# Embedding tower on one core: sixteen tables picked by one-hot matmuls instead of fourteen, the gathers in equal banks, and the dots of three blocks moved in front of the last turns

## The reference

```
e = stack of tbl_f[ids[:, f]] over f          # (512, 32, 128)
dot = einsum('bnd,bmd->bnm', e, e)            # all pairs of features
z = dot[:, iu, ju]                            # the 496 pairs above the diagonal
h = concatenate([z, dense_ctx], axis=1)       # (512, 512)
h = maximum(h @ W_top1 + b_top1, 0)           # 512 -> 512
h = maximum(h @ W_top2 + b_top2, 0)           # 512 -> 256
y = h @ W_top3                                # 256 -> 1
```

## Time and profile before

| | us |
|---|---|
| time of the kernel before, median of 3 runs | 121.43 |
| lowest and highest of them | 121.08, 122.03 |
| span of the profiled execution | 149.4 |
| in it, busy: TensorE matmuls | 118.9 |
| VectorE | 76.3 |
| ScalarE | 79.4 |
| GpSimd | 72.0 |

### The profile page before, as it was taken

The page is one execution under the profiler, slowest core; times in us unless marked ns, Lnnn a source line. Parts: engine busy times, 40 slices in busy tenths (PEclk is TensorE's granted clock), DMA queues, the critical chain, the costliest instruction groups (busy, mean ns, idle before and its releaser), DMA issues.

```text
span 149.4 us, 2614 instructions
## 1 busy us (share of the span) xinstructions
PE 118.9 (80%) x1008; PEld 95.5 (64%) x1008; DVE 76.3 (51%) x106; ACT 79.4 (53%) x128; POOL 72.0 (48%) x80
## 2 busy tenths in 40 slices
PE   0689993599996998798799931289829899999994
PEld 0568871268773875486566721289729788998972
DVE  2999961199969996984969000013103033123411
ACT  3699674199939969999999300030512112210022
POOL 3787777278747747747747777300550720000000
PEclk9999999569999999999999996559986999999999
DMA  4798763136763587379511121102471731015000
GB/s 136 248 335 306 234 207 97 35 61 212 225 205 81 190 263 239 72 241 311 170 35 47 50 55 50 47 0 72 136 222 35 202 77 41 7 35 171 9 0 1
DMA packets 10990, 19.29 MB, mean 129 GB/s; under 512 B 2385, under 2 KB 7377, under 8 KB 10978
## 3 DMA queue, kind: packets, MB, share of 16 engines
q1 hardware_dynamic: 7234, 12.96, 27.9%
q0 software_dynamic: 2304, 4.72, 11.7%
q10 hardware_dynamic: 1440, 1.44, 2.8%
HBM read 17.02 MB, written 2.13 MB: 128 GB/s over the span
## 4 chain that ended last, share of the span: by engine, by line
PE 66%; issue 15%; DVE 11%; ACT 4%; DMA 2%; DVEq 1%; SPq 0%
PE two_ps L562 16%; PE two_ps L564 14%; DVE onehot L327 8%; PE free_ps L604 8%; PE two_ps L623 8%; PE two_ps L604 7%; PE turn_ps L572 4%; DVE low L310 3%; PE free_ps L634 3%; PE two_ps L634 2%; ACT emb L403 2%; DMA home<-picked 2%; PE two_ps L639 1%; PE turn_ps L623 1%; DVEq L364 1%
## 5 line engine op out<-in xcount | busy, mean ns | idle before, releaser
L301 POOL DMA_INDIRECT rows<-tables,row_no x64 | 63.4, 991 | 39.4 <-issue 18.0
L562 PE MATMUL two_ps<-onehot,high 128*128 128x512 f32 x118 | 50.9, 432 | 12.6 <-DVE low L310 5.2
L564 PE MATMUL two_ps<-onehot,low 128*128 128x512 f32 x118 | 48.2, 408 | 1.3 <-issue 1.3
L327 DVE TENSOR_TENSOR onehot<-pick_id,free_ps 128x1536 fp32r<-128x1536 int16 (+2 forms) x25 | 41.5, 1662 | 6.4 <-remote 5.2
L562 PEld LDWEIGHTS two_ps<-onehot,high 128*128 128x128 f32 x118 | 23.4, 198 | 23.7 <-issue 15.1
L564 PEld LDWEIGHTS two_ps<-onehot,low 128*128 128x128 f32 x118 | 23.6, 200 | 5.5 <-issue 1.5
L310 DVE TENSOR_TENSOR low<-home,high 128x512 fp32r<-128x512 f32 (+1 forms) x33 | 20.8, 631 | 8.6 <-issue 6.3
L420 ACT ACTIVATE away<-pick_id,less_row 128x512 f16<-128x512 int16 x34 | 22.3, 712 | 0.0
L604 PE MATMUL free_ps<-emb 128*64 128x64 f32 x272 | 12.7, 231 | 11.8 <-issue 10.5
L435 ACT ACTIVATE onehot<-away 128x512 fp32r<-128x512 f16 x34 | 19.2, 622 | 2.0 <-remote 1.9
L604 PEld LDWEIGHTS free_ps<-emb 128*64 128x64 f32 x272 | 10.7, 140 | 14.0 <-issue 11.9
(11 more groups left out here) (38 smaller groups left out, 63.2 us busy)
## 6 DMA issues: line engine op xcount, KB each, us to landing
home<-picked SPq DMA_DIRECT2D x10, 512.0 KB
home<-picked SPq DMA_DIRECT2D x3, 640.0 KB
pick_id<-pick_ids SPq DMA_DIRECT2D x12, 128.0 KB
w_sb<-w SPq DMA_DIRECT2D x3, 512.0 KB
dot_out<-home SPq DMA_DIRECT2D x10, 128.0 KB, 2.3
rows<-tables,row_no POOLq DMA_INDIRECT x64
dot_out<-home ACTq DMA_DIRECT2D x6, 128.0 KB, 2.5
pairs<-dot_out SPq DMA_DIRECT2D x10, 64.0 KB, 2.0
```

The source lines that it names most:

```text
L301: pool.indirect_dma_start(rows[:, k % ROWS_HELD, i, :], None, lone[i] if one_table else tables, bass.IndirectOffsetOnAxis(ap=id_sb[:, 0, c ...
L327: dve.tensor_tensor(onehot[:, c % HOT:c % HOT + n, :], ids, own, ALU.is_equal).then_inc(onehot_dve, n)
L562: pe.matmul(out, high[:, at, D * k:D * (k + 1)], onehot[:, c % HOT, :], start=(k == 0), stop=False)
L564: pe.matmul(out, low[:, at, D * k:D * (k + 1)], onehot[:, c % HOT, :], start=False, stop=(k == KR[t] - 1)).then_inc(picked_done, 1)
```

## The change

PICK goes from 14 to 16: two more tables of 1250 rows (20 chunks) are picked, and 16 tables are gathered. The leftover banks with their two tensors `lone0` and `lone1` are gone: a block is 4 banks of 4 tiles, 16 banks and 64 gathers in all, and every gather takes its row number from `row_no`. BY_ACT has new numbers for tables 11 to 15: 3, 3, 3, 4, 4 instead of 4, 4, 4. Bank t - 3 (LAG) is turned and copied behind pick t instead of bank t - 1. So banks 0 to 12 are turned among the picks. Dot groups 0 to 5 and `dot(6, 0)` follow right behind with no turns between them, then layer 1 of blocks 0 and 1, and only then turns 13 and 14 and the halves of bank 15, in the places that 17, 18 and 19 had. The same is done on ScalarE. `dot` waits for one bank more with each half group.

```diff
--- before.py
+++ after.py
@@ -8,7 +8,7 @@
         1250, 12500, 1250, 1250, 1250, 12500, 12500, 1000, 1000, 1000, 1250, 1250, 1000, 1000,
         1000, 1250, 1250, 1250]
 
-PICK = 14
+PICK = 16
 PICKED = sorted(range(F), key=lambda f: (ROWS[f], f))[:PICK]
 GATHERED = [f for f in range(F) if f not in PICKED]
 SLOTS = GATHERED + PICKED
@@ -33,7 +33,7 @@
 LOWS = [cut(KR[0], [PIECE])] + [cut(k, LOW_CUT) for k in KR[1:]]
 LOW0 = [sum(len(p) for p in LOWS[:t]) for t in range(PICK + 1)]
 
-BY_ACT = [2, 1, 2, 2, 2, 2, 2, 2, 3, 2, 2, 4, 4, 4]
+BY_ACT = [2, 1, 2, 2, 2, 2, 2, 2, 3, 2, 2, 3, 3, 3, 4, 4]
 
 ALONE, AHEAD = 2, 2
 
@@ -48,13 +48,11 @@
 
 
 TB, SUB = 4, 32
-MORE = GF - 4 * TB
-BANKS = 1 + BLK // SUB
+BANKS = BLK // SUB
 NB = BLOCKS * BANKS
-TILES = [TB if k % BANKS else MORE for k in range(NB)]
-TILE0 = [sum(TILES[:k]) for k in range(NB + 1)]
-
-TURNED = PICK - 1
+TILES = NB * TB
+
+LAG = 3
 TABLES_HELD, IDS_HELD, HOT, AWAY, ROWS_HELD = 3, 4, 16, 8, 4
 
 CTX = 16
@@ -68,7 +66,7 @@
 PARTS = [(0, 2), (2, 3), (3, 4)]
 
 
-def build(nc, row_ids, pick_ids, tables, lone0, lone1, picked, context, w1, w2, small, y):
+def build(nc, row_ids, pick_ids, tables, picked, context, w1, w2, small, y):
     f32, f32r, i32, i16 = mybir.dt.float32, mybir.dt.float32r, mybir.dt.int32, mybir.dt.int16
     ALU = mybir.AluOpType
     ACT = mybir.ActivationFunctionType
@@ -83,10 +81,9 @@
         def sem(name):
             return ctx.enter_context(nc.semaphore(name))
 
-        lone = [lone0, lone1]
         ident = sb("ident", [P, P], f32)
-        id_sb = sb("id_sb", [P, 2, TILE0[NB]], i32)
-        row_no = sb("row_no", [P, TILE0[NB]], i32)
+        id_sb = sb("id_sb", [P, 2, TILES], i32)
+        row_no = sb("row_no", [P, TILES], i32)
         rows = sb("rows", [P, ROWS_HELD, TB, D], f32)
         emb = sb("emb", [P, B, F], f32)
 
@@ -289,18 +286,15 @@
             pool.wait_ge(ident_ready, 1)
             pool.affine_select(out=ident[:, :], in_=ident[:, :], compare_op=ALU.not_equal, fill=1.0,
                                base=0, pattern=[[-1, P]], channel_multiplier=1).then_inc(ident_ready, 1)
-            pool.wait_ge(row_ids_in, 16)
+            pool.wait_ge(row_no_ready, 1)
             for k in range(NB):
-                if k == 1:
-                    pool.wait_ge(row_no_ready, 1)
                 if k >= ROWS_HELD:
                     pool.wait_ge(turned, k - ROWS_HELD + 1)
-                for i in range(TILES[k]):
-                    c = TILE0[k] + i
-                    one_table = k % BANKS == 0
+                for i in range(TB):
+                    c = TB * k + i
                     pool.indirect_dma_start(
-                        rows[:, k % ROWS_HELD, i, :], None, lone[i] if one_table else tables,
-                        bass.IndirectOffsetOnAxis(ap=id_sb[:, 0, c:c + 1] if one_table else row_no[:, c:c + 1], axis=0)
+                        rows[:, k % ROWS_HELD, i, :], None, tables,
+                        bass.IndirectOffsetOnAxis(ap=row_no[:, c:c + 1], axis=0)
                     ).then_inc(late_rows_in if k == NB - 1 and i >= TB // 2 else rows_in[k % ROWS_HELD], 16)
 
         @block.vector
@@ -447,14 +441,8 @@
 
             def emb_out(k):
                 act.wait_ge(turned, k + 1)
-                r, u = divmod(k, BANKS)
-                if u == 0:
-                    out = emb[:, BLK * r:BLK * (r + 1), 4 * TB:GF]
-                    in_ = turn_ps[k % 2][:, 0:MORE * P].rearrange("p (f b) -> p b f", f=MORE)
-                else:
-                    b0 = BLK * r + SUB * (u - 1)
-                    out = emb[:, b0:b0 + SUB, 0:4 * TB].rearrange("p b (i f) -> p i b f", i=TB)
-                    in_ = turn_ps[k % 2][:, :].rearrange("p (i b f) -> p i b f", i=TB, f=4)
+                out = emb[:, SUB * k:SUB * (k + 1), 0:GF].rearrange("p b (i f) -> p i b f", i=TB)
+                in_ = turn_ps[k % 2][:, :].rearrange("p (i b f) -> p i b f", i=TB, f=4)
                 copy(out, in_).then_inc(emb_ready, 1)
 
             def dots_out(grp):
@@ -487,8 +475,8 @@
                     pick_alone(t)
                 elif t % 2:
                     pick_out(t // 2)
-                if t:
-                    emb_out(t - 1)
+                if t >= LAG:
+                    emb_out(t - LAG)
                 if t + 3 < PICK:
                     make_away(t + 3)
                     split_high(t + 3)
@@ -507,17 +495,12 @@
             dots_out(0)
             dots_out(1)
             half_out(0)
-            emb_out(TURNED)
             dots_out(2)
             dots_out(3)
             half_in(0)
-            for k in range(TURNED + 1, NB - 5):
-                emb_out(k)
             half_out(1)
             dots_out(4)
             dots_out(5)
-            emb_out(NB - 5)
-            emb_out(NB - 4)
             half_in(1)
             dots_out(6)
             emb_out(NB - 3)
@@ -565,10 +548,10 @@
                               start=False, stop=(k == KR[t] - 1)).then_inc(picked_done, 1)
 
             def turn(k):
-                pe.wait_ge(rows_in[k % ROWS_HELD], 16 * sum(TILES[k % ROWS_HELD:k + 1:ROWS_HELD]))
+                pe.wait_ge(rows_in[k % ROWS_HELD], 16 * TB * (k // ROWS_HELD + 1))
                 if k >= 2:
                     pe.wait_ge(emb_ready, k - 1)
-                for i in range(TILES[k]):
+                for i in range(TB):
                     last = pe.transpose(turn_ps[k % 2][:, i * P:(i + 1) * P], rows[:, k % ROWS_HELD, i, :], ident[:, :])
                 last.then_inc(turned, 1)
 
@@ -578,7 +561,7 @@
                 if half:
                     pe.wait_ge(late_rows_in, 16 * TB // 2)
                 else:
-                    pe.wait_ge(rows_in[k % ROWS_HELD], 16 * (sum(TILES[k % ROWS_HELD:k + 1:ROWS_HELD]) - TB // 2))
+                    pe.wait_ge(rows_in[k % ROWS_HELD], 16 * (TB * (k // ROWS_HELD + 1) - TB // 2))
                 pe.wait_ge(emb_ready, k - 1 + half)
                 for i in range(2):
                     last = pe.transpose(turn_ps[(k + half) % 2][:, i * P:(i + 1) * P],
@@ -587,8 +570,7 @@
 
             def dot(grp, j):
 
-                r, half = divmod(2 * grp + j, BANKS - 1)
-                pe.wait_ge(emb_ready, BANKS * r + half + 2)
+                pe.wait_ge(emb_ready, 2 * grp + j + 1)
                 if grp >= 2:
                     if j == 0:
                         pe.wait_ge(dots_act, grp - 1)
@@ -643,20 +625,11 @@
             pe.wait_ge(ident_ready, 2)
             for t in range(PICK):
                 pick(t)
-                if t:
-                    turn(t - 1)
-            turn(TURNED)
+                if t >= LAG:
+                    turn(t - LAG)
             pe.wait_ge(pick_emb_ready, TWOS + 1)
-            dot_group(0)
-            dot_group(1)
-            dot_group(2)
-            dot_group(3)
-            for k in range(TURNED + 1, NB - 5):
-                turn(k)
-            dot_group(4)
-            dot_group(5)
-            turn(NB - 5)
-            turn(NB - 4)
+            for grp in range(GROUPS - 2):
+                dot_group(grp)
             dot(6, 0)
             pe.wait_ge(weights_in, 64)
             layer1(0)
@@ -720,7 +693,6 @@
         tiles = []
         for r in range(BLOCKS):
             of = a[BLK * r:BLK * (r + 1)]
-            tiles += [of[:, f] for f in range(4 * TB, GF)]
             tiles += [of[SUB * u:SUB * (u + 1), 4 * i:4 * i + 4].reshape(P) for u in range(BLK // SUB) for i in range(TB)]
         tiles[-TB:] = [of[BLK - SUB + 8 * i:BLK - SUB + 8 * i + 8, 0:4 * TB].reshape(P) for i in range(TB)]
         return np.stack(tiles, axis=1)
@@ -750,8 +722,6 @@
         "pick_ids": np.ascontiguousarray(np.broadcast_to(
             np.ascontiguousarray(ids[:, PICKED].T).view(np.int16)[:, ::2], (P, PICK, B))),
         "tables": np.concatenate([tbl[f] for f in GATHERED[:4 * TB]]),
-        "lone0": tbl[GATHERED[4 * TB]],
-        "lone1": tbl[GATHERED[4 * TB + 1]],
         "picked": np.concatenate([np.pad(tbl[f], ((0, P * k - ROWS[f]), (0, 0))) for f, k in zip(PICKED, KR)]),
         "context": np.ascontiguousarray(context),
         "w1": np.ascontiguousarray(w1.reshape(F, 4, PC, H1).transpose(1, 0, 2, 3).reshape(P, PC, H1)),
```

## The result

The kernel after took 129.56 us (median of 4 runs, 128.27 to 129.70) where the kernel before took 121.63 beside it: slower by 6.35%, ratio 1.0635, 95% interval [1.059, 1.068]. The forecast was 129.2.

A forecast was written before the change was run, and what follows sets the result against it. ScalarE's chain, with VectorE, bounds the picks and TensorE the tail; gathers are covered. Picks +9.2 and behind them −1.4 give +7.8 on 121.43, so 129.2 us (chance 0.58), range 124.5 to 132.5.

The forecast's parts named there:

- The picks, +9.2: Picking stage: with two more tables, ScalarE's count moves its end from 71.9 to 81.1 us.
- Rival 2: Picks afterwards: TensorE alone sets them, ending at 76.4; whole kernel 124.5 us, chance 0.13.
- rivals 2 and 4: The second has its own line; the fourth: gathers bound before, TensorE never waits after, 119.7 us, chance 0.06.
- Behind the picks, −1.4: First dot to end of layer 1 of block 1: dots in one piece shorten 22.5 to 21.1 us.
- the walk: Whole kernel: engine queues followed step by step at the earlier profile's instruction durations, leaving out its waits.
- the two waits that it has: Dots and layer 1, afterwards: dot(6,0) waits 0.8 us for ScalarE's copy, layer1(1) 0.5 for block 1's rows.
- The rest, 0: Turns 13 and 14 and all behind layer 1: same instructions, 23.8 us before and after.
- The gathers, 0: GpSimd's gathers, 72 to 64: covered before the change, so the eight fewer are costed at nothing.
- The cover of 1.4 us: Gathers before the change: the last rows land 1.4 us ahead of the last turn at 98.7.
- the 3.44 of the walk: Gather chain before the change: starts at 3.44 us, then 72 gathers at 1.27 end at 94.9.
- the one that the prediction names: Picks: GpSimd's gathers stand still while VectorE runs two-port operations; the prediction's rows showed nothing of it.
- Things of the profiled execution: First profile: its 28 us above the unprofiled median, TensorE's issue time and late counts, belong to that execution only.

The follow-up runs named there:

- VectorE relieved: Kernel after with the low halves of the last two tables not made by VectorE: 129.03 us, ratio 1.0648 to the kernel before.
- without the eight gathers: Kernel before with the 8 gathers of the leftover banks left out, turns and copies kept on old data: 121.70 us beside 121.91, ratio 0.9992.
- 3, 3, 3 split: Kernel before with the last three tables' one-hots split 3, 3, 3 by ScalarE instead of 4, 4, 4: 121.67 us beside 121.84, ratio 0.9978.
- the two nearest kernels measured: On the chip of 150.9, kernel after with turns 13, 14 and copies back between dots: 0.956; kernel after without twenty low matmuls of the last two tables: 0.953.

## Why the prediction was right

**The picks, +9.2.** In the first profiles of the two kernels without idle stretches, the turn behind the last pick goes from 71.57 to 81.11: +9.5. The step was a count of ScalarE's instructions behind a fixed point with prices from the earlier trace rows, and one length from the earlier trace rows; it hit both ends within 0.3 us. It rested on the claim that VectorE and ScalarE set the stage. For TensorE's side this is shown (4.6 us less work, no gain). That they are far ahead is not so: with VectorE relieved, TensorE became the bound after 1 us. Rival 2's 76.4 for TensorE alone was never in reach: my explanation, argued and not tried, is that TensorE loses time in the early tables that it cannot make up later, since only 16 one-hots and 3 tables are held. (Its sum is 0.5 us short besides: 276 matmuls at 0.232 and 52 tiles at 0.11 are 69.7 us and not 69.2, which moves rivals 2 and 4 by as much and the forecast not at all.)

**Behind the picks, −1.4.** From the first dot to dot(6,1), 1.1 us behind the end of the two layers, the forecast has 23.6 us before and 22.2 after. Measured are 22.2 and 20.9 (two profiles after) and, before, 23.8 without the eight gathers, 24.8 in the 3, 3, 3 split, and 26.05 in the one profile of the kernel before, whose slow clock the ordinary executions do not have. For these, 24.4 is an estimate: 121.9 us, less 1.8 outside, 72.96 to the first dot and 22.7 behind. The same estimate for the kernel after (129.3, 1.8, 82.4, 23.3) gives 21.8. So the gain was about 2.6 us and was put too small by 1.2. Before, the waits of turn 16 for rows (0.8 to 1.0 us) were missing in the walk; after, the two waits that it has (0.8 and 0.5) show in one profile (0.72, and 7.81 for 7.41 in the layers) and not in the other. The price of the order that I had in mind, turns taken out from between dots, is nil.

**The rest, 0.** It went from 22.6 to 22.7 us in the four profiles of the kernel before and its variants to 23.2 or 23.3: +0.6, which I had not. In it the last block's stores take longer: from their issue to that of the loads behind them are 4.1 and 3.8 us in two profiles after (110.92 to 115.04 in the first) and 3.1 in the 3, 3, 3 split. Why was not tried.

**The sum.** By these numbers it is +9.4 to the first dot, −2.6 and +0.6, together +7.4; measured are +7.9 and +7.1. That the forecast of +7.8 came so near is in part luck: a gain too small by 1.2 us stood against a loss of 0.6 and 0.2 of the picks that it did not have.

**The gathers, 0.** Right in time (0.9992), wrong in its working. The cover of 1.4 us was for the last bank, but bank 16, not 19, is the one that is short: its last gather starts at 82.31, where the walk's own prices give 78.4. They start 0.6 us later than the 3.44 of the walk, and they are longer while VectorE is full. The prediction read from the earlier trace rows that they are not. But its window cut the first and last gather off, and two in it are long:

```profile
33.50 1.34 POOL L301 DMA_INDIRECT rows<-tables,row_no  x1 [0.31 <-issue]
35.14 0.95 POOL L301 DMA_INDIRECT rows<-tables,row_no  x1 [0.30 <-issue]
...
40.15 1.49 POOL L301 DMA_INDIRECT rows<-tables,row_no  x1 [0.30 <-issue]
```

In the profile of the kernel before without stretches, the 51 gathers up to the end of the picks take 1.03 us each and the 21 behind it 0.95, none of these over 1.2; that is 4.3 us more for the 51 (an estimate). Whether the cause is the one that the prediction names is not shown; no run took VectorE's work away from them. A part of the gathers that counts about half a microsecond at most and a cost that I called nothing look alike in the sum.

**The reading of the first profile** was the step that failed, though the sum survived it. "Things of the profiled execution" was said of the earlier trace rows; on the chip of 150.9 they are in every execution. The sum was right since it used no wait of that profile, and its scope is the chips without the stretches. For the other kind the forecast would have been wrong in sign for the two nearest kernels measured (−4.4% and −4.7%).

## What to carry to other kernels

When the span of a profile and the timed runs differ by more than a few microseconds, ask for both on one chip before explaining the difference; work from durations and starts, which repeat, and not from the waits. In a stage with three engines within 1 us of each other, relieving one gave at most 1 us here: count all three after the change, and what each holds of the others. Two profiles of one kernel can differ by 1.3 us in a stage (22.2 and 20.9 here), so an agreement to tenths with one of them proves little. Work moved from one path to another has to be priced on its new path first, here 9 us of picking for 10 us of gathering that was hidden.

## What was not expected of the hardware

On one chip TensorE stood still for stretches, with nothing visible to wait for, while indirect DMAs were being issued and short dots were its work: 14 records in 10 us against 166 in 6. Dot(6,0) and layer 1 ran at full pace beside the last three gathers on the same chip, and ScalarE once stood still there for 7.2 us, so neither gathers alone nor TensorE alone describe it; the picks are 10.7 us longer there too. The kernel before took 29 us more (150.9 against 121.9), and 8.2 us went with eight of 72 gathers. On three other chips no profile shows such a stretch; there the kernel before does dot groups 0 to 3 beside gathers at 1.9 us a group (64 records). What the engines lack in these stretches stays open.

Rows fetched by an indirect DMA of 128 rows of 512 bytes landed 2.5 us after their issue in the kernel before (median of 64, its page without stretches), with 4.1 at one place in its chain, and 3.3 us in the kernel after (3.1 in its second profile). The Trainium skill (DMA: Bandwidth & Descriptors, section on the anatomy of one DMA on the SWDGE path) fits a DMA from GpSimd with 2.0 us plus its bytes over 436 GB/s; for these 64 KB that is an estimate of 2.2 us. The kernel before is near it and the kernel after a good microsecond above; the trace decides.
